# A compressed-interaction tower on one core: the last two column tiles split differently, the last merge in halves, and matmuls on constants at both ends

## The chip, the cores and the metric

The kernel runs on one core of one Trainium2 chip. The metric is the device time of one execution in microseconds (us). Three executions of the kernel before took 1251.39, 1255.20 and 1255.94 us, median 1255.2. A further execution was profiled: it took 1253.83 us, and its profile spans 1252.0 us.

## The reference

For 1024 samples, 39 embedding rows of 16 floats are looked up and stacked to `x0` (1024 x 39 x 16). Two layers of a compressed interaction network follow, then an MLP. All in float32:

```python
out = jnp.einsum('bhd,bmd,shm->bsd', xk, x0, W) + b[None, :, None]; relu
x1 = _cin_layer(x0, x0, W1, b1)          # W1 (128, 39, 39)
x2 = _cin_layer(x0, x1, W2, b2)          # W2 (128, 128, 39)
z = concat([x1.sum(-1), x2.sum(-1)], -1) # p1, p2
h = concat([z, dense_ctx], 1)            # 272 wide
h = maximum(h @ W_top1 + b_top1, 0.0); h = maximum(h @ W_top2 + b_top2, 0.0)
y = h @ W_top3
```

## The kernel before, in words

The batch is cut into 8 tiles of 128 samples and the 16 embedding positions d into groups of 4. A **chunk** is one tile with 4 values of d, 512 columns; there are 32 chunks, and each has 4 **column tiles** (ct) of 128 samples with one d, 128 in all.

Layer 1 of chunk f: GpSimd gathers the embedding rows by indirect DMA (L255), SyncE replicates them (L207), PE transposes them (`lift`, L537), they go to DRAM and come back shifted as `z` (L216, L224), VectorE multiplies (`make_f`, L431), PE contracts with W1 (`contract`, L548, seven steps of two records each), ScalarE applies the relu and makes the high part `x1h` (L351, L354), VectorE the low part `x1l` (L436).

Layer 2 of a column tile is on PE three matmuls per **bank** (L564: high x high, high x low, low x high), where a bank is a PSUM bank with up to 4 of the 39 embedding fields m at 128 columns each; there are 10 banks per ct, the last with 3 fields. Five PSUM banks form a ring (`RING`), so bank n can be written when bank n-5 has been read (`wait_bank_free`, L171). What is read out of a bank is multiplied per sample by the embedding value of field m:

- ScalarE takes banks 0, 2, 4, 6, 8 (`A_BANKS`, L33): 20 products of 128x128 per ct into `prod` (L363). GpSimd adds these up: `add_by_transfer` (L266) is a DMA that adds one half of `prod` to the other, then `add_quarters` (L284, 640 columns), `add_inner` (L291, 256), `add_pair` (L296, 128) and `add_last` (L305, 128) make `a_sum`. For the very last ct the transfer is replaced by an add of 1280 columns on GpSimd (`add_first`, L272).
- VectorE takes banks 1, 3, 5, 7, 9: 19 steps per ct that multiply and add into two accumulators `acc` (L470, L468), each one waiting for the step two before it (`v_step`).

`merge(c, n)` on VectorE has three steps per chunk: the two accumulators are added (L479), `a_sum` is added (L483), relu and the sum over d (L490). `fold_p2` (L499) reduces to p2 for a tile.

The order of work on each engine is written out by hand: loops over c (chunk) and g (0 to 39, bank g % 10 of ct g // 10), where layer 1 of chunk c+1 and the merge of chunk c-1 are put at fixed values of g (`MAKE_AT`, `CONTRACT_AT`, `MERGE_AT` = 22, 27, 29 and so on). The merge of the last chunk comes behind all loops, first for three of its four column tiles, then for the last (L520 to L523).

The MLP of the last tile is `mlp_tail`: on PE (L594) it waits for everything but p2, the last five banks of the ring among it, does 16 matmul records that need only p1 and the context (L603, L604), waits for p2 (L605), transposes it (L606), and goes through the three layers (L609, L614, L620), each with ScalarE behind it (L386 to L396).

At the head PE does lift(0), then waits for z and contracts.

Of the kernel before, what the change touches and what calls it, by code (L numbers as in the profile page):

```python
# [9 lines left out]
ALU = mybir.AluOpType  # L10
# [21 lines left out]
BANK_M = [range(MB * k, min(MB * k + MB, M)) for k in range(NB)]  # L32
A_BANKS = (0, 2, 4, 6, 8)  # L33
V_BANKS = tuple(k for k in range(NB) if k not in A_BANKS)
NA, NV = len(A_BANKS), len(V_BANKS)
V_BEFORE = [sum(len(BANK_M[k]) for k in V_BANKS[:i]) for i in range(NV + 1)]
VM = V_BEFORE[NV]
GB = DC * NB
# [9 lines left out]
MERGE_AT = (22, 27, 29)  # L48
FOLD_AT = 36
BATCHES = (range(0, 4), range(4, 7))  # L50
BATCH_IN = (17, 29)
# [23 lines left out]
def build(nc, dram, tables, out):  # L75
    with ExitStack() as ctx:
# [76 lines left out]
        sum3, sum2, sum1, sum0 = sem("sum3"), sem("sum2"), sem("sum1"), sem("sum0")  # L153
        sum_first = sem("sum_first")
        merge_step, p2_done = sem("merge_step"), sem("p2_done")
# [11 lines left out]

        def v_steps(ct, i):
            return ct * VM + V_BEFORE[i]

        def wait_bank_free(eng, n):  # L171
            ct, k = divmod(n - RING, NB)
            if n < RING:
                return
            if k in A_BANKS:
                eng.wait_ge(a_free, ct * NA + A_BANKS.index(k) + 1)
            else:
                eng.wait_ge(v_step, v_steps(ct, V_BANKS.index(k) + 1))

# [63 lines left out]
        def _(pool):  # L243
            def gather(n):
                tile, f = divmod(n, M)
                if f == 0 and tile == 0:
                    pool.wait_ge(in_idx0, 16)
                if f == 0 and tile == 1:
                    pool.wait_ge(in_idx, 16)
                if f == 0 and tile >= E_SLOTS:  # L250
                    last = (tile - E_SLOTS + 1) * CPT * DC
                    pool.wait_ge(v_step, v_steps(last, 0))
                    pool.wait_ge(a_free, last * NA)
# [9 lines left out]
            def add_by_transfer(ct):  # L263
                pool.wait_ge(a_free, (ct + 1) * NA)
                half = 2 * NA * S
                nc.gpsimd.dma_start(products(ct)[:, 0:half], products(ct)[:, half:2 * half], accum_op=ALU.add  # L266
                                    ).then_inc(in_sum[ct % 2], 16)

            def add_first(ct):
                half = 2 * NA * S  # L270
                pool.wait_ge(a_free, (ct + 1) * NA)
                nc.gpsimd.tensor_tensor(products(ct)[:, 0:half], products(ct)[:, 0:half], products(ct)[:, half:2 * half],  # L272
                                        ALU.add).then_inc(sum_first, 1)

            def add_quarters(ct):
                n = NA * S
                if ct < CTS - 1:
                    pool.wait_ge(in_sum[ct % 2], 16 * (ct // 2 + 1))
                else:
                    pool.wait_ge(sum_first, 1)  # L280
                wait(pool, sum0, ct - 1)
# [27 lines left out]
            begun = M  # L309
            for ct in range(CTS):  # L310
                for n in range(begun, M + gathers_before(ct)):
                    gather(n)
                begun = max(begun, M + gathers_before(ct))
                if ct < CTS - 1:
                    add_by_transfer(ct)
                if ct:
# [5 lines left out]
                if ct > 1:  # L322
                    add_last(ct - 2)
            add_pair(CTS - 2)
            add_last(CTS - 2)
            add_first(CTS - 1)
            add_quarters(CTS - 1)
            add_inner(CTS - 1)
            add_pair(CTS - 1)
            add_last(CTS - 1)  # L330

        @block.scalar
        def _(act):
# [22 lines left out]
            def scale_bank(ct, i):  # L356
                k, tile, d = A_BANKS[i], ct // (CPT * DC), ct % D
                act.wait_ge(bank_ready, ct * NB + k + 1)
# [40 lines left out]
            for c in range(-1, CHUNKS):  # L399
                f = c + 1  # L400
                for g in range(GB):
# [8 lines left out]
                    if c >= 0 and g % NB in A_BANKS:  # L410
                        scale_bank(c * DC + g // NB, A_BANKS.index(g % NB))
            mlp_tail()

        @block.vector
        def _(dve):
# [37 lines left out]
            def scale_add_bank(ct, i):  # L453
                k, tile, d = V_BANKS[i], ct // (CPT * DC), ct % D
                c, j = divmod(ct, DC)
# [4 lines left out]
                for n, m in enumerate(BANK_M[k]):  # L460
                    step = V_BEFORE[i] + n
                    src = bank[:, (ct * NB + k) % RING, n * S:(n + 1) * S]
                    scale = emb[:, tile % E_SLOTS, m * D + d:m * D + d + 1]
                    dst = acc[:, c % 2, step % 2, j, :]
                    if step >= 2:
                        dve.wait_ge(v_step, ct * VM + step - 1)
                    if step == 1:
# [5 lines left out]
            def merge(c, n, a=0, b=DC, first=0):  # L473
# [3 lines left out]
                if n == 0:  # L477
                    dve.wait_ge(v_step, v_steps(4 * c + b, 0))
                    nc.vector.tensor_tensor(t_sum[:, a:b, :], acc[:, c % 2, 0, a:b, :], acc[:, c % 2, 1, a:b, :], ALU.add  # L479
                                            ).then_inc(merge_step, 1)  # L480
# [22 lines left out]
            for c in range(-1, CHUNKS):  # L503
                f = c + 1
                for g in range(GB):
                    if c >= 0 and g % NB in V_BANKS:
                        scale_add_bank(c * DC + g // NB, V_BANKS.index(g % NB))
                    if f < CHUNKS and g in MAKE_AT:
# [7 lines left out]
                    if c >= 1 and g in MERGE_AT:  # L516
                        merge(c - 1, MERGE_AT.index(g))
                    if c >= CPT and c % CPT == 0 and g == FOLD_AT:
                        fold_p2(c // CPT - 1)
            for n in range(3):  # L520
                merge(CHUNKS - 1, n, 0, DC - 1)
            for n in range(3):
                merge(CHUNKS - 1, n, DC - 1, DC, 3)  # L523
            fold_p2(TILES - 1)

        @block.tensor
        def _(pe):
            pe.wait_ge(in_ident, 16)

            def lift(f):  # L530
# [63 lines left out]
            def mlp_tail():  # L594
# [27 lines left out]

            lift(0)
            for c in range(-1, CHUNKS):
                f = c + 1
# [50 lines left out]
```

## Time and profile before

| | |
|---|---|
| median of three runs | 1255.2 us (1251.39 to 1255.94) |
| the profiled execution | 1253.83 us, span 1252.0 us |
| PE busy | 1155.7 us, 92% |
| VectorE (DVE) busy | 928.8 us, 74% |
| ScalarE (ACT) busy | 796.9 us, 64% |
| GpSimd (POOL) busy | 848.6 us, 68% |
| mean granted clock of TensorE | 0.989 of 2.4 GHz |

The profile's records give start and duration per instruction or per run of like instructions. PE matmuls are pipelined: records overlap, and the distance between starts is what one costs. An idle time in square brackets stands before the instruction, with what ended it. The granted clock is a share of 2.4 GHz: 0.50 is the lower level, 1.2 GHz. The share of busy time is a mean over the span; the stretches at both ends look different from the middle, where PE is at 9 tenths or more in all 40 slices but the first few.

### The profile page before, as it was taken

To read this page: it belongs to the slowest core of one execution; us is meant where nothing else is said; L and a number is where in the kernel's file an instruction comes from. 1 tells how busy PE (TensorE), PEld (TensorE's weight loads), DVE (VectorE), ACT (ScalarE), POOL (GpSimd) and SP (SyncE) were. 2 spreads that over 40 slices of the span, in tenths; PEclk is the share of its full clock that TensorE was granted. 3 is DMA by queue.
4 is the path that set the end of the run, shared out by engine and by line. 5 is a ranking of instruction groups with operands and counts; after the bars stand their busy time and mean duration, and the time that the engine had idled before them with its cause. 6 is when DMAs were issued, how large, how long until landed. Compare 5 with 4: busy or idle time off the path is not lost.

```text
span 1252.0 us, 17389 instructions
## 1 busy us (share of the span) xinstructions
PE 1155.7 (92%) x4556; PEld 849.7 (68%) x4556; DVE 928.8 (74%) x2846; ACT 796.9 (64%) x2702; POOL 848.6 (68%) x956
## 2 busy tenths in 40 slices
PE   0069999999999999999999999999999999999996
PEld 0037777777777777777776567777777776776775
DVE  2028878887878878788887468888887888774786
ACT  3026766667667766667666466777666666664683
POOL 7725777877787777787786467777777773442455
PEclk9989999999999999999999999999999999999997
DMA  5145666666765666677666267666665676642541
GB/s 163 41 103 106 125 148 130 142 129 134 172 123 119 123 151 125 128 142 151 145 140 121 44 138 156 136 119 124 144 125 124 137 158 133 139 100 62 119 92 35
DMA packets 66346, 154.85 MB, mean 124 GB/s; under 512 B 13219, under 2 KB 18981, under 8 KB 66246
## 3 DMA queue, kind: packets, MB, share of 16 engines
q0 software_dynamic: 28272, 85.81, 36.9%
q1 hardware_dynamic: 37974, 67.92, 22.0%
q8 instruction: 36, 0.59, 0.2%
q14 instruction: 64, 0.52, 0.2%
HBM read 58.59 MB, written 4.20 MB: 50 GB/s over the span
## 4 chain that ended last, share of the span: by engine, by line
POOL 43%; DMA 23%; issue 20%; PE 10%; another core or an unknown queue 2%; ACT 1%; SPq 1%; DVE 0%; POOLq 0%; ACTq 0%; DVEq 0%
DMA prod<-prod 19%; POOL emb L255 15%; POOL tree L284 11%; PE bank L564 7%; POOL tree L291 5%; POOL prod L266 5%; POOL tree L296 3%; POOL a_sum L305 3%; PE l_acc L548 2%; DMA z<-e_shifted 2%; DMA emb_rep<-emb 1%; DMA e_shifted<-e_t 1%; SPq L224 1%; ACT prod L363 0%
## 5 line engine op out<-in xcount | busy, mean ns | idle before, releaser
L363 ACT ACTIVATE prod<-bank,emb 128x128 f32<-128x128 f32 x2560 | 728.6, 372 | 368.8 <-PE bank L564 346.8
L470 DVE SCALAR_TENSOR_TENSOR acc<-bank,emb,acc 128x128 f32<-128x128 f32 x2176 | 613.3, 345 | 138.8 <-PE bank L564 118.4
L564 PE MATMUL bank<-w2h,x1h 128*128 128x512 f32 (+1 forms) x1280 | 537.0, 420 | 5.7 <-DVE x1l L436 4.5
L564 PE MATMUL bank<-w2l,x1h 128*128 128x512 f32 (+1 forms) x1280 | 499.7, 390 | 0.0
L564 PE MATMUL bank<-w2h,x1l 128*128 128x512 f32 (+1 forms) x1280 | 473.6, 433 | 0.0
L255 POOL DMA_INDIRECT emb<-tbl,idx x312 | 309.0, 990 | 82.0 <-issue 77.8
L564 PEld LDWEIGHTS bank<-w2h,x1h 128*128 128x128 f32 x1280 | 242.3, 189 | 119.2 <-issue 54.0
L564 PEld LDWEIGHTS bank<-w2h,x1l 128*128 128x128 f32 x1280 | 241.1, 188 | 87.5 <-issue 35.1
L266 POOL DMA_DIRECT2D prod<-prod x127 | 123.9, 975 | 243.7 <-ACT prod L363 239.7
L284 POOL TENSOR_TENSOR tree<-prod 128x640 f32<-128x640 f32 x128 | 239.3, 1870 | 66.5 <-DMA prod<-prod 66.4
L564 PEld LDWEIGHTS bank<-w2l,x1h 128*128 128x128 f32 x1280 | 241.8, 189 | 60.1 <-issue 17.5
L548 PE MATMUL l_acc<-z,w 117*128 117x512 f32 (+1 forms) x448 | 233.5, 604 | 16.1 <-DVE z L431 12.6
L431 DVE TENSOR_TENSOR z<-e_rep,z 117x512 f32<-117x512 f32 (+1 forms) x224 | 152.9, 684 | 121.0 <-DMA z<-e_shifted 80.3
L291 POOL TENSOR_TENSOR tree<-tree 128x256 f32<-128x256 f32 x128 | 136.7, 1068 | 0.2
L548 PEld LDWEIGHTS l_acc<-z,w 117*128 117x128 f32 (+1 forms) x448 | 84.3, 192 | 43.5 <-DVE z L431 16.7
L296 POOL TENSOR_TENSOR tree<-tree 128x128 f32<-128x128 f32 x128 | 111.3, 870 | 0.1
L305 POOL TENSOR_TENSOR a_sum<-tree 128x128 f32<-128x128 f32 x128 | 89.1, 696 | 0.2
L537 PE MATMUL e_rep<-ident_f,emb_rep 128*117 128x128 f32 x128 | 29.3, 352 | 63.6 <-DMA emb_rep<-emb 63.6
L537 PEld LDWEIGHTS e_rep<-ident_f,emb_rep 128*117 128x117 f32 x128 | 29.0, 287 | 67.7 <-issue 57.9
L470 DVE SCALAR_TENSOR_TENSOR acc<-bank,emb,b_row 128x128 f32<-128x128 f32 x128 | 44.8, 350 | 27.1 <-PE bank L564 25.0
L468 DVE TENSOR_SCALAR acc<-bank,emb 128x128 f32<-128x128 f32 x128 | 44.1, 344 | 0.0
L347 ACT COPY e_t<-e_rep 117x512 f32<-117x512 f32 x32 | 19.5, 611 | 34.7 <-PE e_rep L537 33.8
(75 smaller groups left out, 299.7 us busy)
## 6 DMA issues: line engine op xcount, KB each, us to landing
prod<-prod POOLq DMA_DIRECT2D x127, 640.0 KB
z<-e_shifted SPq DMA_DIRECT2D x160, 234.0 KB
emb_rep<-emb SPq DMA_DIRECT2D x8, 936.0 KB
z<-e_shifted SPq DMA_DIRECT2D x96, 78.0 KB
emb<-tbl,idx POOLq DMA_INDIRECT x312
z<-e_shifted SPq DMA_DIRECT2D x32, 156.0 KB
e_shifted<-e_t SPq DMA_DIRECT2D x32, 128.0 KB, 2.8
prod<-w_by_h SPq DMA_DIRECT2D x3, 832.0 KB
```

What stands on the lines that cost most here:

```text
L255: nc.gpsimd.indirect_dma_start(out=emb[:, tile % E_SLOTS, f * D:(f + 1) * D], out_offset=None, in_=tables[f], in_offset=bass.IndirectOffse ...
L266: nc.gpsimd.dma_start(products(ct)[:, 0:half], products(ct)[:, half:2 * half], accum_op=ALU.add).then_inc(in_sum[ct % 2], 16)
L284: nc.gpsimd.tensor_tensor(tree[:, ct % 2, 0:n], products(ct)[:, 0:n], products(ct)[:, n:2 * n], ALU.add).then_inc(sum3, 1)
L291: nc.gpsimd.tensor_tensor(t[:, 0:n], t[:, 0:n], t[:, n:2 * n], ALU.add).then_inc(sum2, 1)
L296: nc.gpsimd.tensor_tensor(t[:, 0:S], t[:, 0:S], t[:, S:2 * S], ALU.add).then_inc(sum1, 1)
L305: nc.gpsimd.tensor_tensor(a_sum[:, c % 2, j, :], t[:, 0:S], t[:, last:last + S], ALU.add).then_inc(sum0, 1)
L363: last = nc.scalar.activation(prod[:, ct % P_RING, i, n * S:(n + 1) * S], bank[:, (ct * NB + k) % RING, n * S:(n + 1) * S], ACT.Copy, scal ...
L431: nc.vector.tensor_tensor(z[0:rows, f % 2, t, :], e_rep[0:rows, :], z[0:rows, f % 2, t, :], ALU.mult).then_inc(f_made, 1)
L470: nc.vector.scalar_tensor_tensor(dst, src, scale, dst if step else b2_row[:, :], ALU.mult, ALU.add).then_inc(v_step, 1)
L537: last = nc.tensor.transpose(e_rep[0:KP * M, d * P:(d + 1) * P], by_d[:, q * DC + d, :], ident_f[:, :])
L548: nc.tensor.matmul(l1_acc[:, :], w1[0:rows, t, :], z[0:rows, f % 2, t, :], start=(t == 0), stop=(t == NF - 1)).then_inc(f_used, 1)
L564: last = nc.tensor.matmul(out_bank[:, 0:b - a], x, w[:, a:b], start=(n == 0), stop=(n == 2))
```

## The change

The last two column tiles (ct 126 and 127) give ScalarE banks 0, 2 and 4 only; VectorE takes the other seven, 27 steps. For these two, GpSimd adds the 12 products with four adds of its own (`add_twelve`: 768, 384, 128 and 128 columns) without the transfer. Three steps of the last chunk's merge, for its first two column tiles, are done inside the loop at g = 33, 35, 37; the other two column tiles are merged at the end in three steps. PE does 20 matmuls of 128x512 on `w2h` into bank 0 behind lift(0), and 12 into bank 4 in `mlp_tail`, ahead of the wait for p2. The bookkeeping of semaphore counts becomes functions of ct.

```diff
-A_BANKS = (0, 2, 4, 6, 8)
+A_BANKS = ((0, 2, 4, 6, 8), (0, 2, 4))
+V_BANKS = tuple(tuple(k for k in range(NB) if k not in a) for a in A_BANKS)
+LAST = CTS - 2
+WARM_HEAD, WARM_TAIL = 20, 12
+def a_banks(ct):
+    return A_BANKS[ct >= LAST]
...
+MERGE_LAST_AT = (33, 35, 37)
...
-            def add_first(ct):
-                half = 2 * NA * S
-                pool.wait_ge(a_free, (ct + 1) * NA)
-                nc.gpsimd.tensor_tensor(products(ct)[:, 0:half], products(ct)[:, 0:half], products(ct)[:, half:2 * half],
-                                        ALU.add).then_inc(sum_first, 1)
+            def add_twelve(ct):
+                pool.wait_ge(a_free, a_count(ct + 1))
+                wait(pool, sum0, ct)
+                t, src = tree[:, ct % 2, :], products(ct)
+                nc.gpsimd.tensor_tensor(t[:, 0:6 * S], src[:, 0:6 * S], src[:, 6 * S:12 * S], ALU.add).then_inc(sum3, 1)
+                pool.wait_ge(sum3, ct + 1)
+                nc.gpsimd.tensor_tensor(t[:, 0:3 * S], t[:, 0:3 * S], t[:, 3 * S:6 * S], ALU.add).then_inc(sum2, 1)
+                pool.wait_ge(sum2, ct + 1)
+                nc.gpsimd.tensor_tensor(t[:, 0:S], t[:, 0:S], t[:, S:2 * S], ALU.add).then_inc(sum1, 1)
+                pool.wait_ge(sum1, ct + 1)
+                nc.gpsimd.tensor_tensor(a_sum[:, (CHUNKS - 1) % 2, ct % DC, :], t[:, 0:S], t[:, 2 * S:3 * S], ALU.add
+                                        ).then_inc(sum0, 1)
...
-            for ct in range(CTS):
+            for ct in range(LAST):
...
-            add_pair(CTS - 2)
-            add_last(CTS - 2)
-            add_first(CTS - 1)
-            add_quarters(CTS - 1)
-            add_inner(CTS - 1)
-            add_pair(CTS - 1)
-            add_last(CTS - 1)
+            add_pair(LAST - 2)
+            add_last(LAST - 2)
+            add_quarters(LAST - 1)
+            add_inner(LAST - 1)
+            add_pair(LAST - 1)
+            add_last(LAST - 1)
+            for ct in range(LAST, CTS):
+                add_twelve(ct)
...
+                    if c == CHUNKS - 1 and g in MERGE_LAST_AT:
+                        merge(c, MERGE_LAST_AT.index(g), 0, 2)
...
             for n in range(3):
-                merge(CHUNKS - 1, n, 0, DC - 1)
-            for n in range(3):
-                merge(CHUNKS - 1, n, DC - 1, DC, 3)
+                merge(CHUNKS - 1, n, 2, DC, 3)
             fold_p2(TILES - 1)
...
+            def keep_warm(n, bank_ps):
+                pe.wait_ge(w2h_cast, 1)
+                for _ in range(n):
+                    nc.tensor.matmul(bank_ps, w2h[:, 0:P], w2h[:, 0:CH], start=True, stop=True)
...
                     nc.tensor.matmul(tail1[o], wt1[:, 0, o * P:(o + 1) * P], p1[:, a:], start=False, stop=False)
+                keep_warm(WARM_TAIL, bank[:, 4, :])
                 pe.wait_ge(p2_done, TILES)
...
             lift(0)
+            pe.wait_ge(w2l_made, NB)
+            keep_warm(WARM_HEAD, bank[:, 0, :])
```

## Rows read from the trace of the kernel before

**Rows 1.** The page's costliest groups, the first form of the layer-2 matmuls.

```profile
L564 PE MATMUL bank<-w2h,x1h 128*128 128x512 f32 (+1 forms) x1280 | 537.0, 420 | 5.7 <-DVE x1l L436 4.5
```

**Rows 2.** The chain that ended last, 1218 to 1252 us: start, us, what.

```profile
1234.70 2.85 POOL prod L272
...
1243.23 0.49 PE bank L606
...
1250.27 0.25 ACT y L396
```

**Rows 3.** Timeline of VectorE, 1218 to 1252 us: start, us, instruction, count.

```profile
1218.88 0.35 DVE L470 SCALAR_TENSOR_TENSOR acc<-bank,emb,b_row 128x128 f32<-128x128 f32 x1 [0.53 <-PE bank L564]
...
1219.92 1.57 DVE L479 TENSOR_TENSOR t_sum<-acc 128x512 f32<-128x512 f32 x1
...
1225.89 2.44 DVE L490 SCALAR_TENSOR_TENSOR p2acc<-t_sum,p2acc 128x512 f32<-128x512 f32 x1
...
1228.76 4.47 DVE L470 SCALAR_TENSOR_TENSOR acc<-bank,emb,acc 128x128 f32<-128x128 f32 x17
...
1234.80 3.15 DVE L483 TENSOR_TENSOR t_sum<-t_sum,a_sum 128x384 f32<-128x384 f32 x1 [0.95 <-POOL a_sum L305]
...
1242.16 1.02 DVE L499 TENSOR_REDUCE p<-p2acc 128x128 f32<-128x512 f32 x1
```

**Rows 4.** All instructions of line L483: durations in ns, min/median/max, forms.

```profile
L483 DVE TENSOR_TENSOR t_sum<-t_sum,a_sum x33: 293/682/3154, 147.2 to 1241.5; 128x512 f32<-128x512 f32 x31, 128x384 f32<-128x384 f32 x1, 128x128 f32<-128x128 f32 x1
```

**Rows 5.** Timeline of GpSimd, 1230 to 1234 us.

```profile
1230.35 1.58 POOL L284 TENSOR_TENSOR tree<-prod 128x640 f32<-128x640 f32 x1 [0.65 <-DMA prod<-prod]
...
1232.30 0.73 POOL L291 TENSOR_TENSOR tree<-tree 128x256 f32<-128x256 f32 x1
```

**Rows 6.** Timeline of PE's matmuls, 1228 to 1252 us.

```profile
1230.45 0.39 PE L564 MATMUL bank<-w2h,x1h 128*128 128x512 f32 x1
1230.68 0.40 PE L564 MATMUL bank<-w2l,x1h 128*128 128x512 f32 x1
...
1233.38 0.46 PE L603 MATMUL e_rep<-ctx_t,wt 16*128 16x128 f32 x2 [1.09 <-DVE acc L470]
1233.77 0.49 PE L604 MATMUL e_rep<-p,wt 128*128 128x128 f32 x2
...
1236.16 0.79 PE L603 MATMUL bank<-ctx_t,wt 16*128 16x128 f32 x2
1236.88 0.80 PE L604 MATMUL bank<-p,wt 128*128 128x128 f32 x2
...
1245.92 3.47 PE L614 MATMUL bank<-h,wt 128*128 128x128 f32 x16
```

**Rows 7.** Slices of 1 us at the end: slice, length, PE busy (count), granted clock, DMA.

```profile
1235.00:1236.00 1.00, 1.00 (x5) 0.72 0.00 0
...
1249.00:1250.00 1.00, 0.82 (x7) 0.95 0.00 0
```

**Rows 8.** Timeline of PE's matmuls at the head, 56 to 95 us.

```profile
57.56 1.18 PE L537 MATMUL e_rep<-ident_f,emb_rep 128*117 128x128 f32 x4 [57.56 <-DMA emb_rep<-emb]
65.61 2.08 PE L548 MATMUL l_acc<-z,w 117*128 117x512 f32 x2 [6.87 <-DVE z L431]
70.19 7.75 PE L548 MATMUL l_acc<-z,w 117*128 117x512 f32 x12 [2.50 <-issue]
...
83.15 0.77 PE L564 MATMUL bank<-w2h,x1h 128*128 128x512 f32 x1 [4.51 <-DVE x1l L436]
...
85.00 0.63 PE L564 MATMUL bank<-w2h,x1h 128*128 128x512 f32 x1
85.43 0.63 PE L564 MATMUL bank<-w2l,x1h 128*128 128x512 f32 x1
```

**Rows 9.** Slices of 1 us at the head, columns as in rows 7.

```profile
88.00:89.00 1.00, 1.00 (x5) 0.71 0.71 158
```

**Rows 10.** Timeline of VectorE at the head, 56 to 84 us.

```profile
72.76 1.88 DVE L431 TENSOR_TENSOR z<-e_rep,z 117x512 f32<-117x512 f32 x3 [1.43 <-issue]
```

More of the change, by code:

```diff
@@ L32, with v_banks, a_count, v_count @@
 BANK_M = [range(MB * k, min(MB * k + MB, M)) for k in range(NB)]
-A_BANKS = (0, 2, 4, 6, 8)
[L34 to L37, printed above, removed]
+A_BANKS = ((0, 2, 4, 6, 8), (0, 2, 4))
+V_BANKS = tuple(tuple(k for k in range(NB) if k not in a) for a in A_BANKS)
+NA = len(A_BANKS[0])
+LAST = CTS - 2
+WARM_HEAD, WARM_TAIL = 20, 12
+def a_banks(ct):
+    return A_BANKS[ct >= LAST]
+def v_banks(ct):
+    return V_BANKS[ct >= LAST]
+def a_count(ct):
+    return sum(len(a_banks(x)) for x in range(ct))
+def v_count(ct, i=0):
+    return (sum(len(BANK_M[k]) for x in range(ct) for k in v_banks(x))
+            + sum(len(BANK_M[k]) for k in v_banks(ct)[:i]) if ct < CTS else
+            sum(len(BANK_M[k]) for x in range(CTS) for k in v_banks(x)))
 GB = DC * NB
@@ L174, in wait_bank_free @@
                 return
-            if k in A_BANKS:
-                eng.wait_ge(a_free, ct * NA + A_BANKS.index(k) + 1)
+            if k in a_banks(ct):
+                eng.wait_ge(a_free, a_count(ct) + a_banks(ct).index(k) + 1)
             else:
-                eng.wait_ge(v_step, v_steps(ct, V_BANKS.index(k) + 1))
+                eng.wait_ge(v_step, v_count(ct, v_banks(ct).index(k) + 1))
         block = ctx.enter_context(nc.Block())
@@ L251, in gather @@
                     last = (tile - E_SLOTS + 1) * CPT * DC
-                    pool.wait_ge(v_step, v_steps(last, 0))
-                    pool.wait_ge(a_free, last * NA)
+                    pool.wait_ge(v_step, v_count(last))
+                    pool.wait_ge(a_free, a_count(last))
                     pool.wait_ge(lifted, (tile - E_SLOTS + 1) * CPT)
@@ L267, in add_by_transfer @@
                                     ).then_inc(in_sum[ct % 2], 16)
-            def add_first(ct):
-                half = 2 * NA * S
-                pool.wait_ge(a_free, (ct + 1) * NA)
-                nc.gpsimd.tensor_tensor(products(ct)[:, 0:half], products(ct)[:, 0:half], products(ct)[:, half:2 * half],
-                                        ALU.add).then_inc(sum_first, 1)
+            def add_twelve(ct):
+                pool.wait_ge(a_free, a_count(ct + 1))
+                wait(pool, sum0, ct)
[8 more added lines that the diff above has]
+                                        ).then_inc(sum0, 1)
             def add_quarters(ct):
                 n = NA * S
[L277 to L280, printed above, removed]
+                pool.wait_ge(in_sum[ct % 2], 16 * (ct // 2 + 1))
                 wait(pool, sum0, ct - 1)
@@ L313, in _ @@
                 begun = max(begun, M + gathers_before(ct))
-                if ct < CTS - 1:
-                    add_by_transfer(ct)
+                add_by_transfer(ct)
                 if ct:
@@ L356, in scale_bank @@
             def scale_bank(ct, i):
-                k, tile, d = A_BANKS[i], ct // (CPT * DC), ct % D
+                k, tile, d = a_banks(ct)[i], ct // (CPT * DC), ct % D
                 act.wait_ge(bank_ready, ct * NB + k + 1)
@@ L409, in _ @@
                                 mlp(BATCH_IN.index(c), step)
-                    if c >= 0 and g % NB in A_BANKS:
-                        scale_bank(c * DC + g // NB, A_BANKS.index(g % NB))
+                    ct, k = c * DC + g // NB, g % NB
+                    if c >= 0 and k in a_banks(ct):
+                        scale_bank(ct, a_banks(ct).index(k))
             mlp_tail()
@@ L453, in scale_add_bank @@
             def scale_add_bank(ct, i):
-                k, tile, d = V_BANKS[i], ct // (CPT * DC), ct % D
+                k, tile, d = v_banks(ct)[i], ct // (CPT * DC), ct % D
                 c, j = divmod(ct, DC)
@@ L460, in scale_add_bank @@
                 for n, m in enumerate(BANK_M[k]):
-                    step = V_BEFORE[i] + n
+                    step = v_count(ct, i) - v_count(ct) + n
                     src = bank[:, (ct * NB + k) % RING, n * S:(n + 1) * S]
@@ L465, in scale_add_bank @@
                     if step >= 2:
-                        dve.wait_ge(v_step, ct * VM + step - 1)
+                        dve.wait_ge(v_step, v_count(ct) + step - 1)
                     if step == 1:
@@ L477, in merge @@
                 if n == 0:
-                    dve.wait_ge(v_step, v_steps(4 * c + b, 0))
+                    dve.wait_ge(v_step, v_count(4 * c + b))
                     nc.vector.tensor_tensor(t_sum[:, a:b, :], acc[:, c % 2, 0, a:b, :], acc[:, c % 2, 1, a:b, :], ALU.add
@@ L505, in _ @@
                 for g in range(GB):
-                    if c >= 0 and g % NB in V_BANKS:
-                        scale_add_bank(c * DC + g // NB, V_BANKS.index(g % NB))
+                    ct, k = c * DC + g // NB, g % NB
+                    if c >= 0 and k in v_banks(ct):
+                        scale_add_bank(ct, v_banks(ct).index(k))
                     if f < CHUNKS and g in MAKE_AT:
```

3 lines of the change are left out of this document (removed).

## The prediction

> **What bounds the kernel now.** I read the page's table of groups first. The layer-2 matmuls (L564) stood idle 5.7 us in 1280 of their first form, and 4.5 us of that is one wait, for the first x1l at the head [rows 1]: between about 83 and 1228 us the kernel runs at TensorE's pace. An edit pays there only if it takes work off PE or stalls it less. The change touches the two ends, so the rest is read by stretch.
>
> The chain of waits of the last 34 us runs through GpSimd: the direct add of the last column tile's products (2.85 us), its tree, then the last merge on VectorE, and PE's transpose of p2 at 1243.23 [rows 2]. But VectorE is close behind. It works without a gap from 1218.88, when column tile (ct) 126 begins for it, to the last product at 1233.23 [rows 3]. Those 14.35 us are 38 steps at 0.258 us, which is (4.47 - 0.34)/16 from the row of 17, so 9.8 us; three merge steps of chunk 30, 0.6 us each where nothing holds them, 1.8 us; and 2.7 us in which merge steps stood still. The last shows as durations of 1.57 and 2.44 us in place of the 0.68 that a step not held takes, and a 384-column one took 3.15 us beside the 2.85 us add: it began 0.14 us after that add and ended 0.4 us after it [rows 2 to 4]. A merge step has two operands in SBUF; one that meets a GpSimd add waits for the add's end. The product steps, which read PSUM, kept their 0.258 us throughout.
>
> PE ends the last bank and waits for VectorE's last product (1.09 us, row of 1233.38). It then does 16 small matmuls of the MLP that don't need p2: pairs 0.39 to 0.42 us apart at first, 0.72 us apart later (1236.16 to 1236.88) [rows 6]. Between the two the granted clock fell from 2.4 to 1.2 GHz, and it came back in the slice from 1249 us only, when nearly all was done [rows 7]. From the transpose to the end of the y copy takes 7.3 us at half clock [rows 2].
>
> **Part 1, the three banks.** ScalarE's two banks per ct were worth 8 products; VectorE takes them, so it has 27 steps per ct in place of 19, 54 in the last two. Counted from 1218.88: 54 x 0.258 = 13.9; the three merge steps of chunk 30, 1.8; the three half merges now inside ct 127, 256 columns each, between 0.29 us (128 columns) and 0.68 us (512) [rows 4], I take 0.4 each, 1.2; stalls behind GpSimd as before, 2.7; and those of the three new steps. These are bounded by nothing and by a whole GpSimd instruction each (1.9, 1.1 and 0.5 us, priced below, 3.5 together); I take 1.6, the middle, since GpSimd is busy with ct 126 and 127 just then. Sum 21.2 us: VectorE's last product moves from 1233.2 to **1240.1 us**. Ends: with 1.0 us of stalls in all, 1236.8; with all of them, 1242.0.
>
> Queued behind these steps are the ring's banks. With 1.03 us of VectorE per bank against 0.70 us of PE (three matmuls at 0.23), four V banks in a row outrun the ring of five: PE waits some 1 us before bank 3 of ct 127 and as much before bank 6, and still ends its last bank near 1233.4. ScalarE has nothing to lose, GpSimd's waits on `a_free` come sooner.
>
> **Part 2, the tree.** A GpSimd add costs 1.58 us for 640 columns and 0.73 for 256 [rows 5], 2.2 ns a column: 768 columns 1.86, 384 columns 1.01, 128 columns 0.45. So add_twelve is 1.86 + 1.01 + 0.45 + 0.45 and three gaps of 0.07, 4.0 us. That replaces, for ct 126, a transfer with its descriptor work and a tree, and for ct 127 7.0 us of adds. The one for 127 can start when ScalarE has done its third bank, about 1230, and when 126's is through, about 1231.5, and ends near 1236. GpSimd is no longer last; VectorE is.
>
> **Part 3, the end of the merge.** What is left behind the last product is three steps of 256 columns, no longer held by GpSimd (1.3 us) and the fold (1.02) [rows 3]: p2 is ready at 1242.4 against 1243.2 now. Taken alone the split and the halves give 0.8 us; with the ends above, between 4.1 gained and 1.1 lost.
>
> **Part 4, the constants at the tail.** PE's queue is in order, and the small matmuls wait for all five last banks, hence for VectorE's last product. This was 1233.2 and is now 1240.1. Behind it stand 8 pairs, then the 12 new matmuls, then the transpose. PE has been idle about 6.7 us by then, so it starts at 1.2 GHz: 8 x 0.72 = 5.8 us. A 512-column matmul is 0.43 us at 1.2 GHz (from 85.00 to 85.43) and 0.23 at 2.4 [rows 6, 8]: the twelve cost 5.1 or 2.8 us. The clock rose about 5.5 us after work began at 83.15 and about 5.9 us after 1243.23 [rows 7, 9]. If the pairs count as work, it rises at about 1245.6, with the last pair, and the twelve end at 1248.5. That is 6 us after p2 is ready: the transpose moves from 1243.2 to **1248.5**, 5.3 us later.
>
> What is bought for that: at full clock the rest goes faster. The 24 matmuls of 128 columns on p2t and h1 take 0.22 us each now [rows 6]; by the pairs above (0.41 against 0.72) they come to 0.12, and as ScalarE's h1 activations then set part of the pace I take 2.7 of the 5.1 us away, and 0.4 for the transpose and the last four matmuls. The stretch is 7.3 - 3.1 = 4.2 us, and y is written at 1252.7 against 1250.52: **+2.2 us**.
>
> The Trainium skill, "TensorE: Matmul & The Clock Gate", section "Back-to-back issue gap", gives about 131 ns per 512-column matmul in a sustained stream; by it the twelve would be 1.6 us and the tail +1.0. The trace's own 0.23 us is used.
>
> **Part 5, the constants at the head.** They stand between lift(0), over at 58.74, and the first contraction. Twenty at half clock take 8.5 us, and less if the clock rises underway: they end between 65.5 and 67.3. The contraction of group 0 starts at 65.61 now, so it may slip by up to 1.7 us, but the next starts at 70.19 only, when its z is there, which hides that [rows 8]. Would it find a fast PE? Its matmuls now run at half clock until about 75 (12 in 7.75 us). With full clock, the last three operands come from VectorE from 72.76 on [rows 10], the last at 74.6; the contractions then end near 76.0 instead of 77.8, **1.8 us** gained, and PE is the pace from there on. But between the twenty and 70.19 PE is idle some 3.5 us but for one contraction. In the trace the clock was gone after 4.5 us of idleness (83.15 starts slow), and at 1235 it fell after only 1.1 us of idleness and thin work [rows 6 to 8]. I take nothing gained as likelier, and both as close. The same 4.5 us wait ahead of 83.15 stays, with its slow 5.5 us.
>
> The same page's section "Loop structure matters more than you think" says that bursts with waits between them start slow each time; by that rule the head's matmuls give 0 here rather than 1.8 us. No row shows a filled gap, so it is open.
>
> **Sum.** 1253.83 (this profiled execution: span 1252.0 and 1.8 around it) + 2.2 - 0 = **1256.0 us**. The execution is 1.4 us below the median of the three (1255.2), inside their spread of 4.5, so I take nothing off or on for that. One measurement of this kernel can tell about 0.5%, 6.3 us, from no change.
>
> **Rivals.**
> *The end stays hot and short* (faster). If VectorE's merge steps meet few GpSimd adds, the last product is at 1236.8, and if the clock is held or returns at once, PE needs 8 x 0.41 + 2.8 = 6.1 us, transpose at 1242.9, y at 1247.1: 3.4 us gained, with the head's 1.8 in all 5.2, 1248.6 us. For it: stalls of a merge were only 0 to 2 us each. Against it: PE idle for over 3 us even then, and 1235's fall after 1.1.
> *The twelve run cold on the path* (slower). If the small pairs don't count as work, as 1235 suggests, where the clock fell while they ran, it stays at 1.2 GHz through 5.8 + 5.1 us: transpose at 1251.0. The rest takes 4.2 to 7.3 us, y at 1255.2 to 1258.3, +4.7 to +7.8, so 1258.5 to 1261.6. It decides once VectorE's last product is later than 1235.4: 1250.5 less 10.9 and 4.2 (1232.3 with 7.3); it is put at 1240.1. For it: the fall at 1235. Against it: at half clock the same pairs fill the array twice as much of the time.
> *Nothing to see.* The head's matmuls die in the gap and the tail's cost and gain cancel (a clock back a little early, VectorE at 1238.5): 1253 to 1255.
>
> **How the numbers follow.** The forecast, with the head's gain or without, 1254.2 to 1257: 0.45. Cold on the path: 0.27, of which about half passes 1260.1, that is +0.5%. Nothing to see: 0.15. Hot and short: 0.13, of which less than half passes 1247.5. So slower by over 0.5%: 0.15; faster: 0.06; within: 0.79. The range holds all but the ends of the two outer cases, and half a microsecond for the spread of the runs: 1248.0 to 1262.0.
>
> **What would show it.** Right: VectorE's last L470 near 1240; GpSimd's last add near 1236; the first L603 held until VectorE's end; the granted clock at 0.5 when it starts; p2's fold near 1242 and PE's transpose 4 us or more after it, released by nothing but PE's own queue; L614's 16 matmuls in 2 to 2.5 us; at the head, 20 matmuls ending near 66 and the contractions from 70.19 at 0.85 us each at first. Wrong: the transpose directly behind the fold; VectorE's end before 1237; contractions at 0.43 us from 70.19; anything that changes between 100 and 1200 us.

## The result and the profile after

The changed kernel took 1259.68 us in the median of 20 executions (1253.88 to 1264.18), the kernel before 1252.96 (1247.68 to 1257.46): ratio 1.0049, 95% interval 1.0034 to 1.0063, that is 4 to 8 us slower. The forecast was 1256.0 us in 1248.0 to 1262.0, with +2.2 us against its own profile. The profiled execution of the changed kernel took 1255.82 us, span 1254.0, so it is one of the short ones: the two spans differ by 2.0 us only.

The page's row of PE's first form answers to [rows 1].

```profile
PE 1165.2 (93%) x4588; PEld 854.8 (68%) x4588; DVE 931.7 (74%) x2862; ACT 793.9 (63%) x2686; POOL 848.3 (68%) x954
...
L594 PE MATMUL bank<-w2h,x1h 128*128 128x512 f32 (+1 forms) x1280 | 536.9, 419 | 6.3 <-DVE x1l L460 5.9
```

The 32 added matmuls are PE's x4588 against x4556. The mean of one layer-2 matmul is as before (419 ns, 420 before); the one wait at the head has grown from 4.5 to 5.9 us.

VectorE at the end, the timeline of the changed kernel (L494 and L492 are the product steps, L503, L507 and L514 the merge, L523 the fold), against [rows 3]:

```profile
1218.33 0.35 DVE L494 SCALAR_TENSOR_TENSOR acc<-bank,emb,b_row 128x128 f32<-128x128 f32 x1 [0.53 <-PE bank L594]
...
1219.37 1.58 DVE L503 TENSOR_TENSOR t_sum<-acc 128x512 f32<-128x512 f32 x1
...
1227.42 0.67 DVE L514 SCALAR_TENSOR_TENSOR p2acc<-t_sum,p2acc 128x512 f32<-128x512 f32 x1
...
1230.09 1.09 DVE L503 TENSOR_TENSOR t_sum<-acc 128x256 f32<-128x256 f32 x1
...
1234.55 1.02 DVE L514 SCALAR_TENSOR_TENSOR p2acc<-t_sum,p2acc 128x256 f32<-128x256 f32 x1
1235.49 1.89 DVE L494 SCALAR_TENSOR_TENSOR acc<-bank,emb,acc 128x128 f32<-128x128 f32 x7
...
1238.87 1.02 DVE L523 TENSOR_REDUCE p<-p2acc 128x128 f32<-128x512 f32 x1
```

The last product ends at 1237.38, 19.05 us after VectorE's start on ct 126 (14.35 before), and p2 is ready at 1239.89, 21.6 us after it (24.3 before). GpSimd, same stretch, against [rows 5]:

```profile
1226.89 0.46 POOL L328 TENSOR_TENSOR a_sum<-tree 128x128 f32<-128x128 f32 x1
1227.50 2.31 POOL L292 TENSOR_TENSOR tree<-prod 128x768 f32<-128x768 f32 x1
1229.89 1.01 POOL L294 TENSOR_TENSOR tree<-tree 128x384 f32<-128x384 f32 x1
...
1232.19 2.03 POOL L292 TENSOR_TENSOR tree<-prod 128x768 f32<-128x768 f32 x1
...
1235.96 0.46 POOL L298 TENSOR_TENSOR a_sum<-tree 128x128 f32<-128x128 f32 x1
```

GpSimd is done at 1236.4, before VectorE. So the split worked: counted from VectorE's start on ct 126, p2 comes 2.7 us sooner. PE does not use it. PE's timeline, against [rows 6], and its clock in slices of 1 us, against [rows 7]:

```profile
1237.53 0.76 PE L633 MATMUL e_rep<-ctx_t,wt 16*128 16x128 f32 x2 [5.46 <-DVE acc L494]
...
1242.56 0.80 PE L634 MATMUL bank<-p,wt 128*128 128x128 f32 x2
1243.01 4.80 PE L569 MATMUL bank<-w2h 128*128 128x512 f32 x12
1247.65 0.27 PE L637 MATMUL bank<-ident_f,p 128*128 128x128 f32 x1
...
1249.27 2.00 PE L645 MATMUL bank<-h,wt 128*128 128x128 f32 x16
```

```profile
1236.00:1237.00 1.00, 0.00 (x0) 0.82 0.00 0
1237.00:1238.00 1.00, 0.47 (x2) 0.50 0.00 0
...
1246.00:1247.00 1.00, 1.00 (x4) 0.56 0.00 0
```

PE waits 5.46 us for VectorE's last product, starts at 1.2 GHz, needs 5.8 us for the small pairs (the 16 records of L633 and L634, two to a pair) and 4.3 more until the twelve are through (1247.65 is the start of the transpose), all while p2 lies ready since 1239.89. The transpose has no wait in front of it, so it is held by PE's own queue. From its start to the end of y's copy, the last row of ScalarE, it is 4.8 us in place of 7.3:

```profile
1252.18 0.26 ACT L419 COPY y<-bank 1x128 f32<-1x128 f32 x1 [0.47 <-PE bank L651]
```

I measure the ending from VectorE's first step of ct 126 to the end of y's copy, which takes the middle out: 31.6 us before (1218.88 to 1250.52), 34.1 us after (1218.33 to 1252.44), **+2.5 us**.

The head, PE's timeline, against [rows 8]:

```profile
58.40 6.68 PE L569 MATMUL bank<-w2h 128*128 128x512 f32 x20
65.58 1.12 PE L578 MATMUL l_acc<-z,w 117*128 117x512 f32 x2 [0.50 <-DVE z L455]
70.52 8.18 PE L578 MATMUL l_acc<-z,w 117*128 117x512 f32 x12 [3.82 <-issue]
...
85.27 0.77 PE L594 MATMUL bank<-w2h,x1h 128*128 128x512 f32 x1 [5.86 <-DVE x1l L460]
```

The twenty did bring the clock up: the first contraction takes 1.12 us in place of 2.08. In the gap behind it the clock fell, and it came back only in the middle of the contractions. Slices of 1 us, against [rows 9]:

```profile
69.00:70.00 1.00, 0.00 (x0) 0.65 0.93 148
...
76.00:77.00 1.00, 1.00 (x4) 0.94 0.00 0
```

This column has to be read with care at the head. In the profile of the kernel before it says 1.00 until 81 us, although the contractions from 71.21 to 74.62 start 0.85 us apart, as at 1.2 GHz, and those from 75.20 on 0.43: ahead of the first change that a profile records, go by the distances of the records.

The contractions end at 78.70 (77.94 before). Then ScalarE starts the relu 4.42 us later, where it was 3.06 us before (77.94 to 81.00); the profile says "remote" for both and names no engine or transfer. Timeline of ScalarE, the kernel before and then the changed one:

```profile
81.00 0.66 ACT L351 ACTIVATE l_acc<-l_acc,bias 128x512 f32<-128x512 f32 x1 [21.58 <-remote]
81.70 0.58 ACT L354 CAST x1h<-l_acc 128x512 fp32r<-128x512 f32 x1
```

```profile
83.12 0.66 ACT L374 ACTIVATE l_acc<-l_acc,bias 128x512 f32<-128x512 f32 x1 [23.69 <-remote]
83.81 0.59 ACT L377 CAST x1h<-l_acc 128x512 fp32r<-128x512 f32 x1
```

The first x1h is begun at 83.81, against 81.70: the head is 2.1 us slower in this pair of profiles. From there to the last x1h the changed kernel took 1112.4 us and the one before 1115.1; the edit does not touch that middle, and its 2.7 us hide the head's share in the spans.

### The profile page after: what moved, and what is told of

Read it like the earlier page. It is cut to its first block, busy times and chain, and to the rows that moved or that the text cites. A ratio compares the mean times of both kernels' runs of the same rounds, so it can differ in the third digit from the quotient of the medians.

```text
span 1254.0 us, 17456 instructions
## 1 busy us (share of the span) xinstructions
PE 1165.2 (93%) x4588; PEld 854.8 (68%) x4588; DVE 931.7 (74%) x2862; ACT 793.9 (63%) x2686; POOL 848.3 (68%) x954
## 4 chain that ended last, share of the span: by engine, by line
POOL 33%; PE 25%; DMA 22%; issue 14%; another core or an unknown queue 2%; ACT 2%; DVE 2%; SPq 1%; POOLq 0%; ACTq 0%; DVEq 0%
PE bank L594 18%; DMA prod<-prod 17%; POOL emb L274 13%; POOL tree L307 8%; PE l_acc L578 4%; POOL tree L314 4%; POOL prod L285 4%; POOL tree L319 2%; POOL a_sum L328 2%; DMA z<-e_shifted 2%; DMA emb_rep<-emb 1%; DVE acc L494 1%; DMA prod<-w_by_h 1%; PE misc L613 1%
## 5 line engine op out<-in xcount | busy, mean ns | idle before, releaser
L494 DVE SCALAR_TENSOR_TENSOR acc<-bank,emb,acc 128x128 f32<-128x128 f32 x2192 | 616.7, 343 | 135.9 <-PE bank L594 121.7
L307 POOL TENSOR_TENSOR tree<-prod 128x640 f32<-128x640 f32 x126 | 235.6, 1870 | 69.1 <-DMA prod<-prod 69.1
L494 DVE SCALAR_TENSOR_TENSOR acc<-bank,emb,b_row 128x128 f32<-128x128 f32 x128 | 44.5, 348 | 27.0 <-PE bank L594 25.0
L492 DVE TENSOR_SCALAR acc<-bank,emb 128x128 f32<-128x128 f32 x128 | 43.8, 342 | 0.0
```

The source lines that it names most:

```text
L307: nc.gpsimd.tensor_tensor(tree[:, ct % 2, 0:n], products(ct)[:, 0:n], products(ct)[:, n:2 * n], ALU.add).then_inc(sum3, 1)
L494: nc.vector.scalar_tensor_tensor(dst, src, scale, dst if step else b2_row[:, :], ALU.mult, ALU.add).then_inc(v_step, 1)
```

## The experiments

Theory A: the loss is PE's order at the tail; the small pairs and the twelve stand behind VectorE's last product. Rivals: the split itself costs; constants cost wherever they are; something outside the ending costs. Each run was timed in five rounds beside the kernel before on the same chip. Since the middle varies by 14 us between profiles (1109 to 1124 us from first to last x1h), the ending, counted as above, is the sharper measure. It repeats to some tenths: 34.1, 34.6 and 34.5 us in three profiles of the changed kernel, 31.6 and 31.0 in the two with the tail of the kernel before (before and e4). A difference under 0.7 us is not read.

| run | ratio to before (95%) | ending, us | first x1h, us |
|---|---|---|---|
| before | | 31.6 | 81.7 |
| changed | 1.0049 (1.0034 to 1.0063) | 34.1 | 83.8 |
| e1_split_only | 0.9960 (0.9936 to 0.9983) | 32.0 | 78.7 |
| e2_no_tail_warm | 0.9982 (0.9957 to 1.0006) | 32.2 | 80.3 |
| e3_before_tail_warm | 0.9991 (0.9963 to 1.0019) | 29.3 | 78.1 |
| e4_before_head_warm | 0.9978 (0.9953 to 1.0002) | 31.0 | 78.6 |
| f1_changed_again | 1.0008 (0.9984 to 1.0031) | 34.6 | 79.3 |
| f2_small_first | 0.9962 (0.9938 to 0.9985) | 27.9 | 79.3 |
| f3_tail_warm_only | 1.0019 (0.9997 to 1.0040) | 34.8 | 78.8 |
| f4_head_filled | 0.9988 (0.9964 to 1.0011) | 32.0 | 77.2 |
| g1_changed_third | 1.0031 (1.0009 to 1.0053) | 34.5 | 83.9 |
| g2_both_filled | 1.0006 (0.9984 to 1.0028) | 32.1 | 84.4 |
| g3_interleaved | 0.9966 (0.9938 to 0.9993) | 32.1 | 81.3 |
| g4_small_first_none | 0.9962 (0.9932 to 0.9992) | 28.6 | 80.8 |

The e, f and g runs were on one chip each, three in all. The last two columns come from one profiled execution per run, the ratio from all.

**The two sets of constants taken away.** e1:

```diff
-WARM_HEAD, WARM_TAIL = 20, 12
+WARM_HEAD, WARM_TAIL = 0, 0
```

> The changed kernel with no matmuls on constants at either end: the three-bank split, add_twelve and the half merges alone. Theory A (the twelve at the tail are the loss): VectorE's last product near 1237.4 and p2 near 1239.9 as in the changed kernel, but PE's eight pairs start at VectorE's last product at half clock and end 5.8 us later, so the transpose is at about 1243.3, as before the change, and the ending takes 7.3 us at half clock: about 1251, within 1 us of the kernel before, 5 us below the median of the changed one if the head costs something, 2 us if it does not. Theory B (the split itself costs, by putting VectorE behind): 3 us or more above the kernel before with both sets of constants gone.

e2 keeps the head's: `WARM_HEAD, WARM_TAIL = 20, 0`.

> The changed kernel without the twelve at the tail, with the twenty at the head. Theory A: transpose 4.4 us earlier than in the changed kernel, about 5.8 us behind VectorE's last product, ending 7.3 us in place of 4.8; net 2 us below the changed kernel. Against the run without either, it shows the head alone: 0 if the head's matmuls do nothing, +2 us if the later first x1h of the changed kernel's profile (83.8 against 81.7) is their doing.

PE's timeline of e1 at the end:

```profile
1231.08 0.76 PE L633 MATMUL e_rep<-ctx_t,wt 16*128 16x128 f32 x2 [5.46 <-DVE acc L494]
...
1236.11 0.80 PE L634 MATMUL bank<-p,wt 128*128 128x128 f32 x2
1236.70 0.42 PE L637 MATMUL bank<-ident_f,p 128*128 128x128 f32 x1
...
1239.34 3.35 PE L645 MATMUL bank<-h,wt 128*128 128x128 f32 x16
```

The wait of 5.46 us and the half clock are the same, and the transpose starts 5.6 us behind the first pair in place of 10.1. VectorE's fold ended at 1233.43, so even the pairs alone are 3.3 us late. The endings of e1 and e2 are 32.0 and 32.2 us: the split with its halves brings nothing and costs nothing there, as what it gains on VectorE is eaten up by PE's wait; theory B (3 us or more) falls. e1 was timed 0.4% faster than the kernel before, which its ending does not explain (below). e2's first x1h is 1.6 us later than e1's, of which 0.8 us is z being ready later (contractions from 71.11 against 70.28) and 0.8 us slower contractions (8.49 us for 7.71).

**The constants added to the kernel before.** e3 adds `keep_warm(12, bank[:, 4, :])` ahead of the wait for p2, e4 `keep_warm(20, bank[:, 0, :])` behind lift(0), each with the helper and nothing else.

> The kernel before with the twelve added at the tail, nothing else. Theory A: PE waits from 1237.7 to 1243.2 there, and twelve at half clock take 5.1 us, so they end by 1242.8 and delay nothing; the clock comes back during them and the ending takes 4.8 us in place of 7.3: 2 to 3 us faster than the kernel before. Rival (constants cost wherever they are, or do not bring the clock back in time): 0 or slower.

> The kernel before with the twenty added at the head, nothing else. Theory C (the head's matmuls change nothing that counts): contractions from 70.2 at half clock, since the clock falls in the gap; first x1h within 0.5 us of 81.7; ratio 1.000. Rival D (they cost): the fall of the clock comes in the middle of the contractions' start, first x1h 2 us later, ratio 1.0015 to 1.003. Rival E (they help): contractions at 0.86 us a pair, first x1h near 80, ratio 0.998.

PE's timeline of e3 at the end:

```profile
1232.33 5.47 PE L544 MATMUL bank<-w2h 128*128 128x512 f32 x12
1238.60 0.33 PE L612 MATMUL bank<-ident_f,p 128*128 128x128 f32 x1 [0.81 <-DVE p L499]
...
1240.28 2.00 PE L620 MATMUL bank<-h,wt 128*128 128x128 f32 x16
```

Here the transpose waits for the fold, 0.81 us: the twelve fit into a wait that is there anyway, the clock is back by 1238, and L620's sixteen take 2.00 us in place of 3.47. The ending is 29.3 us, 2.4 less than before and 1.7 less than e4, which has the same tail without the twelve. The same twelve gain or lose by what they stand behind. The timing (0.9991) neither shows nor excludes that. In e4 the contractions took 7.66 us against 7.75, as theory C has it; the clock had fallen at 68 us and was back at 74.8. Its ending of 31.0 us, with the tail unchanged, shows how much that measure moves by when the clock comes back: at 1242.1 there, 4.4 us behind the transpose's start, where it was 5.9 before.

**The changed kernel again, and without the head.** f1 is the changed kernel, f3 has `WARM_HEAD, WARM_TAIL = 0, 12`.

> The changed kernel itself, beside the others on one chip. From VectorE's first step of ct 126 to y it took 34.1 us in its profile, against 31.6 before, 32.0 without both sets of constants, 32.2 without the twelve, 29.3 with the twelve added to the kernel before. Theory A (all of the difference is in that ending): ratio to the kernel before 1.002 (+2.5 us). Theory F (something outside the ending costs as well, as the first measurement's 1.0049 and the 0.9960 of the run without constants suggest): ratio 1.004 or more here too, and then its profile differs from the others before ct 126.

> The changed kernel without the head's twenty, twelve at the tail kept. Theory A: 34.1 us from ct 126 to y as in the changed kernel, 2 us over the run without both; ratio about 1.002. Theory F: if the head is what costs, this is 2 us or more below the changed kernel of the same call.

Endings of 34.6 and 34.8 us: the twelve behind VectorE's last product cost 2.6 to 2.8 us against e1's 32.0, with or without the head's twenty. f3 is no faster than f1, so on this chip the head's twenty are not what costs.

**Small pairs first.** f2, with `WARM_HEAD, WARM_TAIL = 0, 12`; g4 is the same with `0, 0`:

```diff
-                for n in range(CTS * NB, CTS * NB + RING):
-                    wait_bank_free(pe, n)
+                wait_bank_free(pe, CTS * NB)
...
-                keep_warm(WARM_TAIL, bank[:, 4, :])
+                wait_bank_free(pe, CTS * NB + 1)
+                keep_warm(WARM_TAIL, bank[:, 1, :])
+                for n in range(CTS * NB + 2, CTS * NB + RING):
+                    wait_bank_free(pe, n)
```

> The changed kernel without the head's twenty; at the tail the eight small pairs wait only for the one bank that they write (bank 5 of ct 127), the twelve write the next slot and wait for bank 6, and the waits for the last three banks come after. Theory A (PE's order, small pairs and twelve behind VectorE's last product, is the loss): pairs start near ct-126 start + 14, at full clock, the twelve end before p2 is ready (21.6 us after ct 126's start), the transpose follows the fold at once, and the ending takes 4.8 us where the clock is held, 7.3 where not: 26.4 to 28.9 us from ct 126 to y, ratio 0.996 to 0.998 against the kernel before. Rival: the clock falls anyway, since pairs and a short train do not hold it, and the gain is under 2.7 us.

> Small pairs first, no constants at either end. This shows what the constants at the tail are worth once they stand on no path: p2 ready 21.6 us after ct 126's start, transpose at once, the ending at half clock 7.3 us: 28.9 us from ct 126 to y, against 27.9 with the twelve behind the pairs. So nearly all that the small pairs' place gives (31.9 to 28.9, 3 us) comes without constants. Ratio 0.9975. Rival: the clock does not fall when nothing stands behind the pairs, ending 4.8 us, 26.4 in all.

PE's timeline of f2, then VectorE's fold there:

```profile
1233.53 0.45 PE L632 MATMUL e_rep<-ctx_t,wt 16*128 16x128 f32 x2 [0.28 <-DVE acc L494]
...
1237.16 5.47 PE L569 MATMUL bank<-w2h 128*128 128x512 f32 x12
1242.42 0.41 PE L639 MATMUL bank<-ident_f,p 128*128 128x128 f32 x1
```

```profile
1240.04 1.05 DVE L523 TENSOR_REDUCE p<-p2acc 128x128 f32<-128x512 f32 x1
```

The pairs wait 0.28 us in place of 5.46. The clock still fell, at 1236 (0.52 in that slice), so the twelve ran at 1.2 GHz and ended 1.3 us behind the fold, and brought the clock back in time for the rest: 27.9 us, 6.2 us less than the changed kernel. Without them (g4) the transpose is released by the fold, and the rest is at half clock: 28.6 us. PE's timeline of g4:

```profile
1234.59 0.45 PE L632 MATMUL e_rep<-ctx_t,wt 16*128 16x128 f32 x2 [0.29 <-DVE acc L494]
...
1242.26 0.45 PE L639 MATMUL bank<-ident_f,p 128*128 128x128 f32 x1 [3.65 <-DVE p L523]
```

Both were timed 0.9962, with intervals below 1. The sharpest pair is f2 against f3: on one chip, with the same constants, they differ in PE's order at the tail alone, and took 1246.30 and 1254.02 us in the median, with intervals that do not meet. That is 7.7 us, and 6.9 between their endings. So PE's order was the loss. What the constants add to its repair, 0.7 us between these two profiles, is no more than the ending moves by itself, and is not shown.

One profile does not stand for all executions here. The mean granted clock of each is on record, and 0.001 of it is 2.5 us at 1.2 GHz. In f2 it was 0.995 for the profiled execution but 0.999 or 1.000 in three of the twelve, which leaves under 4 us at 1.2 GHz (the stretch ahead of the first recorded change aside), where the fall at the tail alone lasted 6.8 us in the profile. So the clock did not always fall as it does there. In g4 none of the twelve was above 0.995.

**The gap at the head filled.** f4, with `WARM_HEAD, WARM_TAIL = 20, 0` and:

```diff
                         contract(f, CONTRACT_AT.index(g))
+                        if f == 0 and g == CONTRACT_AT[0]:
+                            keep_warm(14, bank[:, 0, :])
```

> The changed kernel without the twelve at the tail; at the head twenty as in the change, and fourteen more behind the first contraction, in the gap where the clock fell. Theory A (the gap undoes the twenty): with the gap filled, contractions run at 0.86 us a pair from 70.2 and end near 76, the first x1h is at 76.7 to 77.2 in place of 78.7, and the first banks are at full clock. Rival: z lands before the fourteen are through and they delay the contractions, or they do not hold the clock: x1h at 78.5 or later.

PE's timeline of f4 at the head:

```profile
70.39 2.84 PE L578 MATMUL l_acc<-z,w 117*128 117x512 f32 x6 [0.52 <-DVE z L455]
73.61 2.85 PE L578 MATMUL l_acc<-z,w 117*128 117x512 f32 x6 [0.37 <-DVE z L455]
76.29 0.87 PE L562 MATMUL e_rep<-ident_f,emb_rep 128*117 128x128 f32 x4
```

Now the contractions run at full clock, 6 in 2.85 us, and wait for z in between. They end at 76.46 and x1h is at 77.2, 1.5 to 2.1 us sooner than in e1, f2 and f3 (about 1 us sooner than in e3, the earliest of those without constants at the head): the gap was what undid the twenty. The time did not resolve it (0.9988).

**Both ends, and the interleaved tail.** g3 has no constants at the head, waits for two banks and puts three matmuls on constants behind each two pairs; g2 is g3 with f4's head.

```diff
-                for n in range(CTS * NB, CTS * NB + RING):
-                    wait_bank_free(pe, n)
+                wait_bank_free(pe, CTS * NB)
+                wait_bank_free(pe, CTS * NB + 1)
...
-                keep_warm(WARM_TAIL, bank[:, 4, :])
+                    keep_warm(WARM_TAIL // 4, bank[:, 1, :])
+                for n in range(CTS * NB + 2, CTS * NB + RING):
+                    wait_bank_free(pe, n)
```

> The same at the tail alone, no constants at the head. Theory (thin pairs let the clock fall, in 1235 before the change and 1236 with small pairs first): with three 512-column matmuls behind each two pairs the granted clock stays at 1.0 through the tail, twelve and pairs take 6 to 6.5 us in place of 8.7, and end by the time p2 is ready: 26.4 to 26.8 us from ct 126 to y. Rival (the fall comes from the idle time before the pairs): it falls as before, the constants run at 0.43 us and end 2 us behind p2: 28 us or more. Ratio 0.996 and 0.997.

> The changed kernel with what the runs so far suggest: at the head twenty and fourteen (contractions at full clock, first x1h at 77.2 in place of 78.7 to 79.3), at the tail the small pairs waiting for two banks only and each two pairs followed by three matmuls on constants. The ending is expected at 26.4 us from ct 126 to y (p2 ready after 21.6, 4.8 at full clock), 5.2 less than before; with the head's 1.5 to 2 some 7 us in all: ratio 0.9945. Rival: the clock falls in the pairs as in the run with the twelve behind them, and the ending is 28 us, ratio 0.996.

PE's timeline of g2 at both ends, and its clock at the second:

```profile
70.20 2.58 PE L578 MATMUL l_acc<-z,w 117*128 117x512 f32 x5 [0.33 <-issue]
75.00 1.01 PE L578 MATMUL l_acc<-z,w 117*128 117x512 f32 x1 [2.22 <-issue]
77.09 1.01 PE L578 MATMUL l_acc<-z,w 117*128 117x512 f32 x1 [1.08 <-issue]
79.19 4.48 PE L578 MATMUL l_acc<-z,w 117*128 117x512 f32 x5 [1.09 <-issue]
...
1238.53 0.46 PE L633 MATMUL e_rep<-ctx_t,wt 16*128 16x128 f32 x2 [1.66 <-DVE acc L494]
1238.91 0.77 PE L634 MATMUL e_rep<-p,wt 128*128 128x128 f32 x2
1239.34 1.63 PE L569 MATMUL bank<-w2h 128*128 128x512 f32 x3
```

```profile
1238.00:1239.00 1.00, 0.47 (x3) 0.99 0.00 0
1239.00:1240.00 1.00, 1.00 (x4) 0.50 0.00 0
```

My theory that the thin pairs let the clock fall did not hold in these two profiles: it fell 0.5 us after the first pair began, behind a wait of 1.66 us, and in g3 after 0.8 us. That the wait is the cause is not shown either, since in f2 and g4 it fell 2.5 and 2.4 us after pairs that had waited 0.3 us only. Interleaved constants did not keep the clock, nor did they bring it back: PE worked without a gap for over 9 us more, and the clock rose at 1252.6 only (1256.9 in g3), among the matmuls behind the transpose. Each three constants then cost 1.3 us on the path, so the ending was 32.1 us in both. But g3's profiled execution is its longest, 1262.48 us against a median of 1252.20, and has the lowest mean clock of its twelve, 0.988; another had 0.999 and took 1241.20. So whether the clock falls differs from one execution to the next, and g3's ending is that of a bad one. How PE could be kept at 2.4 GHz there, say by constants in the waits of 0.7 and 1.66 us ahead of the pairs, was not tried. At the head, g2's contractions stood still between records for 1 to 2 us, three times, with no releaser, and ended at 83.67 us: what the filled gap gave in f4 was lost in this profile to pauses that f4 did not have.

**The changed kernel a third time.**

> The changed kernel once more. Its ending is 34.1 and 34.6 us from ct 126 to y in two profiles, against 31.6 before: 1.002 by that. The two timings said 1.0049 (1.0034 to 1.0063) and 1.0008 (0.9984 to 1.0031). If the rest of the first is the spread of the long middle, this lies between, near 1.002 to 1.003; if it is a cost that the profiles do not show, 1.004 or more.

1.0031, and an ending of 34.5 us. Its head is that of the first profile of the changed kernel: x1h at 83.9 behind a pause of 4.46 us between contraction and relu. On this third chip the kernels without constants at the head had pauses too, of 1.4 and 1.9 us (x1h at 80.8 and 81.3), as the first profile of the kernel before (3.06 us); on the chips of the e and f runs no kernel had more than 0.05 us. So where the pause occurs, kernels with the twenty alone were 2.1 to 3.1 us later at x1h (two profiles against three), and 0.65 us on average where it does not (79.3, 80.3 and 78.6 against 78.7, 78.1, 79.3 and 78.8, which overlap). With the ending's 2.5 to 2.9 us this makes 4.6 to 6 us or 3.1 to 3.6: the first fits 1.0049 and 1.0031, the second 1.0008 within its interval. That is a reading of few profiles. What ends the pause is not shown.

Against the endings alone, the timings of e1 and g3 are about 0.4% too low (their intervals leave out 1.0003), and that of the changed kernel too high; the other ten agree. For g3 the profiled execution's ending is no measure of the others, as said above. The e1 difference stays unexplained; nothing in its profile but the middle's own spread could hold it.

## Why the prediction was right, and where only by luck

The direction and the place were right: the twelve and the pairs on PE behind VectorE's last product, the transpose late by its own queue, nothing from the head, +2.2 us forecast against +2.5 in the ending. Point by point:

- **Part 1.** Forecast 21.2 us from VectorE's start on ct 126 to its last product, measured 19.05. The products were right (54 x 0.258 = 13.9). The failed term is the stalls, taken as 2.7 + 1.6: merge steps lasted 1.58, 0.67 and 0.67 us, and in the halves 1.09, 0.41 and 1.02, which leaves 2.2 us of stalls where 4.3 were taken. "Stalls as before" did not hold for the 2.44 us step: between its adds for ct 125 and those for ct 126 GpSimd now was idle for 0.15 us (1227.35 to 1227.50), the step began in that gap at 1227.42 and ran in 0.67. It did so in all eleven profiles with the split, against 2.43 to 2.44 in the three without. (The rival's "0 to 2 us each" overlooks the step of 3.15 us, which was held some 2.6.)
- **Part 2.** The twelve products took 4.2 to 4.5 us (forecast 4.0, with the 768-column add at 2.0 to 2.3 rather than 1.86) and ended at 1236.4 (near 1236).
- **Part 3.** p2 ready 2.7 us sooner, where 0.8 was forecast, in the range given of 4.1 gained to 1.1 lost.
- **Part 4.** The eight pairs at half clock were 5.8 us, as forecast. The step that failed is "if the pairs count as work, the clock rises with the last pair": it rose 9.4 us after the pairs began, 3.9 us into the denser work, and the twelve took 4.3 us in place of 2.8. In the six other profiles with this order (e1, e2, f1, f3, f4, g1) it rose 10.3 to 11.8 us after the first pair, and 4.5 to 5.4 us after denser work began. The rival's mechanism (the twelve cold, on the path) is the one that took place; with VectorE 2.2 us earlier than forecast it came out at the forecast's time. Two errors of about 2 us cancelled: that much was luck. (The terms 1240.1, 5.8 and 2.8 add up to 1248.7, not 1248.5, which changes nothing.)
- **The rest behind the transpose** took 4.8 us, forecast 4.2. The 128-column matmuls at full clock are 0.11 to 0.12 us apart as reckoned. The 24 of them with ScalarE's steps between gave back 2.3 us where 2.7 was taken, the transpose and the last four matmuls 0.2 where 0.4 was.
- **Part 5.** Nothing gained at the head was taken as likelier, and it held: the gap undid the twenty, and in f4's profile filling it gave 1.0 to 2.1 us where 1.8 was reckoned. That the twenty could cost was not priced: in the changed kernel the clock came back at 76, where the contractions ran at half clock until about 75 before. They took 8.2 to 8.5 us in four of five profiles with the twenty, and 7.4 to 7.9 in six of seven without.
- **The time.** The profile gave +2.0 in span and the 20 runs 0.49%, 6.1 us. The ending's 2.5 us is shown; the head's 2 us is what one pair of profiles says, supported by g1; the remaining 1 to 2 us is open.

## What to carry to other kernels

Before an engine's wait is filled with work, ask what the wait is behind in that queue: twelve matmuls on constants gained 1.7 to 2.4 us of the ending behind early work and cost 2.6 to 2.8 behind late work. When load moves to the engine that ends last, look for instructions on a third engine that wait for its last result though they need an earlier one; here that was a wait for five banks where one would do, and it was worth 3.4 us with no constants at all. And a profile's span is a poor judge of 2 us under a middle that varies by 14; measure from the last common point, and ask of the profiled execution whether its time and mean clock are like those of the others.

## What the runs showed of the hardware

- The clock can fall soon after a short wait: in g2 0.5 us and in g3 0.8 us after PE resumed from 1.66 us of idleness, in the kernel before 2.1 us after it resumed from 1.09 us [rows 6, 7], in f2 and g4 2.5 and 2.4 us after 0.3 us.
- The small pairs, 5.8 us of them at 1.2 GHz without a gap, did not bring the clock back in any of seven profiles, nor did two pairs and three 512-column matmuls in turn, over 9 us of them in g2 and g3. Twelve 512-column matmuls in a row did within 3.9 to 5.7 us of their start (six profiles), and the MLP's 128-column ones behind the transpose within 2.9 to 5.4 us (eight profiles). The Trainium skill, "TensorE: Matmul & The Clock Gate", section "What's actually happening", says that the clock comes from how busy PE has been. The profile calls PE busy at 1.00 in every full slice of the pairs, so the busy share that it prints does not tell whether the clock will rise.
- VectorE's merge steps are held by GpSimd's adds one at a time: 0.67 us unheld for 512 columns, 3.15 us for 384 columns beside an add of 2.88 us [rows 3, 4]. A gap of 0.15 us on GpSimd at the right time took 1.8 us from one of them.
